# Quotients of cross attention's outputs formed by POOL behind its subtraction, DVE's block transpose of them near the end of its slot

## The reference

```python
def _L0_xattn_ref(Q, K, V, mask, Wq, bq, Wk, bk, Wv, bv, Wo, bo):     # 16 heads of 8
    q = _split(Q @ Wq.T + bq, N_HEAD)
    k = _split(K @ Wk.T + bk, N_HEAD)
    v = _split(V @ Wv.T + bv, N_HEAD)
    score = jnp.einsum('bhqd,bhkd->bhqk', q, k) * scale
    score = jnp.where(mask == 0, -jnp.inf, score)
    attn = jax.nn.softmax(score, axis=-1)
    out = jnp.einsum('bhqk,bhkd->bhqd', attn, v)
    B, H, S, dh = out.shape
    out = out.transpose(0, 2, 1, 3).reshape(B, S, H * dh)
    return out @ Wo.T + bo
...
x = x + _L0_xattn_ref(_layernorm(x, axis=-1), ctx_1024, ctx_1024, mask, ...)   # x: (128, 32, 128), ctx: (128, 257, 128)
```

## Time and profile before

| | |
|---|---|
| median of 3 runs | 1475.41 us (1472.41 to 1478.68) |
| the profiled execution | 1479.32 us, its span 1477.5 us, granted clock 0.948 of full |
| cross attention in it | POOL's first subtraction starts at 63.29 us, its last at 476.94 us |
| PE busy | 1314.1 us, 89% |
| DVE busy | 1195.3 us, 81% |
| ACT busy | 1113.4 us, 75% |
| POOL busy | 716.2 us, 48% |

### The profile page before, as it was taken

How to read it: one execution, slowest core, us unless ns; L and a number is a source line. 1 busy time by engine, 2 the same in 40 slices (tenths; PEclk the granted TensorE clock), 3 DMA queues, 4 the chain that set the end, 5 groups by cost and what they waited for, 6 DMA issues and landing times.

```text
span 1477.5 us, 45922 instructions
## 1 busy us (share of the span) xinstructions
PE 1314.1 (89%) x15671; PEld 997.7 (68%) x15671; DVE 1195.3 (81%) x3413; ACT 1113.4 (75%) x1877; POOL 716.2 (48%) x557
## 2 busy tenths in 40 slices
PE   5898999999978799679788798999999998998988
PEld 3676778777766688537566566666767666666666
DVE  4799899899997689678886886878787878687885
ACT  3698999999967567368767676778787787677776
POOL 7276777787769445514322232343444433233323
PEclk9999999999986699789989999999999999999999
DMA  6876676677642688100000000000000000000000
GB/s 162 220 209 164 185 193 179 186 193 186 176 117 66 171 211 213 36 1 2 1 0 0 0 2 1 0 0 0 0 0 0 0 0 1 2 7 14 7 14 15
DMA packets 196200, 108.45 MB, mean 73 GB/s; under 512 B 89740, under 2 KB 194028, under 8 KB 196076
## 3 DMA queue, kind: packets, MB, share of 16 engines
q1 hardware_dynamic: 122032, 84.65, 20.9%
q10 hardware_dynamic: 74044, 22.17, 6.8%
HBM read 67.62 MB, written 39.03 MB: 72 GB/s over the span
## 4 chain that ended last, share of the span: by engine, by line
DVE 20%; PE 15%; issue 12%; ACT 5%; DVEq 1%; ACTq 0%
PE pair L1739 7%; PE pair L1721 6%; DVE hs L1652 4%; ACT gf L1594 3%; ACT gh L1599 2%; DVE xc L1626 2%; DVE rs L51 1%; PE pair L1751 1%; DVE rs L53 1%; DVE gl L1638 1%; DVE st L1617 1%; DVE rs L49 1%; DVE rs L38 1%; DVE mv L1621 1%; PE pair L1728 1%
## 5 line engine op out<-in xcount | busy, mean ns | idle before, releaser
L1581 POOL TENSOR_TENSOR gl<-gf,gh 128x1024 f16<-128x1024 f32 x128 | 289.9, 2265 | 554.2 <-ACT gh L1599 554.2
L1594 ACT ACTIVATE gf<-pair,b1c 128x512 f32<-128x512 f32 x512 | 327.1, 680 | 151.9 <-PE pair L1721 151.7
L1739 PE MATMUL pair<-w2p,gh 128*128 (+1 forms) x4096 | 369.0, 222 | 9.0 <-DVE gl L1638 9.0
L1739 PE MATMUL pair<-w2p,gl 128*128 (+1 forms) x2048 | 360.0, 222 | 0.0
L1739 PEld LDWEIGHTS pair<-w2p,gh 128*128 128x128 f16 x4096 | 328.2, 100 | 35.1 <-issue 7.8
L1721 PE MATMUL pair<-xh,w1p 128*128 128x512 f16 x1024 | 328.7, 382 | 3.0 <-DVE w2p L1368 2.9
L404 POOL TENSOR_TENSOR pl<-p,ph 128x1024 f16<-128x1024 f32 x128 | 272.8, 2131 | 119.3 <-ACT ph L461 119.1
L1599 ACT ACTIVATE gh<-gf 128x1024 f16<-128x1024 f32 x256 | 270.6, 1057 | 25.5 <-ACT gf L1594 2.4
L1638 DVE SCALAR_TENSOR_TENSOR gl<-gf,gh 128x1024 f16<-128x1024 f32 x128 | 167.7, 1310 | 126.1 <-ACT gh L1599 124.0
L1739 PEld LDWEIGHTS pair<-w2p,gl 128*128 128x128 f16 x2048 | 204.3, 100 | 0.0
L1721 PE MATMUL pair<-xl,w1p 128*128 128x512 f16 x512 | 196.0, 383 | 0.0
(11 more groups left out here) (232 smaller groups left out, 2489.4 us busy)
## 6 DMA issues: line engine op xcount, KB each, us to landing
KS<-k_parts_dram SPq DMA_DIRECT2D x64, 384.0 KB, 4.5
k_parts_dram<-kh SPq DMA_DIRECT2D x64, 256.0 KB, 3.2
cx<-in_ctx_dram ACTq DMA_DIRECT2D x30, 512.0 KB, 4.5
k_parts_dram<-kl SPq DMA_DIRECT2D x64, 128.0 KB, 3.7
w1p<-in_L_ffn_w_dram SPq DMA_DIRECT2D x8, 512.0 KB, 5.9
w2p<-in_L_ffn_w_dram SPq DMA_DIRECT2D x8, 512.0 KB, 7.8
QS<-q_parts_dram ACTq DMA_DIRECT2D x128, 24.0 KB
Q<-q_parts_dram SPq DMA_DIRECT2D x32, 96.0 KB
```

What stands on the lines that cost most here:

```text
L1581: pool.tensor_tensor(gl[u.m2][:, 0:h, :], gf[u.m2][:, 0:h, :], gh[u.m2][:, 0:h, :], ALU.subtract).then_inc(d_loP, 1)
L1594: act.activation(gf[u.m2][:, c, :], hb[c][:, :], ACT.Gelu, scale=1.0 / WS, bias=b1c[:, u.step.expert(u.e), c]).then_inc(d_g, 1)
L1739: last = pe.matmul(yb[v.m2][:, t * D:(t + 1) * D], g[:, c, t * P:(t + 1) * P], w2p[:, le, part, c, :].rearrange("p a h -> p (a h)"), start ...
```

## The change

POOL gets one more instruction in each odd slot from 5 to 131: the quotients `on`, as a `tensor_tensor` multiply of the same tiles, placed behind its subtraction of the slot. DVE loses the quotients, and its block transpose of them moves from before the reduce to behind it. The computation is the same.

```diff
@@ POOL, slot s, behind pl
                         pool.tensor_tensor(pl[n % 4][:, :, :], p32[n % 2][:, :, :], ph[n % 4][:, :, :],
                                            ALU.subtract).then_inc(pl_done, 1)
+                    m = half(s - 5)
+                    if m is not None:
+                        pool.wait_ge(rec_done, m + 1)
+                        if m >= 2:
+                            pool.wait_ge(ot_done, m - 1)
+                        pool.tensor_tensor(on[m % 2][:, :, :, :], osum[m % 2][:, :, :, 0:DH],
+                                           orec[m % 2][:, :, :].unsqueeze(3).broadcast_to((P, 2, G, DH)),
+                                           ALU.mult).then_inc(on_done, 1)
@@ DVE
-                def quotients(m):
-                    dve.wait_ge(rec_done, m + 1)
-                    dve.scalar_tensor_tensor(on[m % 2][:, :, :, :], osum[m % 2][:, :, :, 0:DH], 1.0,
-                                             orec[m % 2][:, :, :].unsqueeze(3).broadcast_to((P, 2, G, DH)),
-                                             ALU.mult, ALU.mult).then_inc(on_done, 1)
...
-                    if m is not None:
-                        quotients(m)
                     if y is not None:
                         dve.wait_ge(y_read, y + 1)
                         dve.bn_stats(st2[:, y, :], xs[:, y, :]).then_inc(c_st, 1)
-                    if m is not None:
-                        transposed_quotients(m)
...
                         dve.tensor_reduce(mx[n // PB % 2][:, :, n % PB], RB[:, :].rearrange("p (g k) -> p g k", g=G),
                                           AX.X, ALU.max, negate=True).then_inc(r_read, 1)
+                    if half(s - 5) is not None:
+                        transposed_quotients(half(s - 5))
```

## The result

| | median us | lowest to highest | runs |
|---|---|---|---|
| before | 1474.42 | 1472.41 to 1478.68 | 4 |
| after | 1588.83 | 1585.90 to 1589.86 | 4 |

The account below looks back on a forecast made before the run. PE, ACT and DVE were nearly full; the wait that ends last decides, in a closed loop of one pair. Loop +90, layer norm steps +1 and end +7 made +98 us; against 1475.4 that gave 1574 us, range 1540 to 1630.

Parts of the forecast that it names:

- The wait and its place: DVE's transpose behind the reduce waits for POOL in every odd slot, 1.8 to about 2.8 us, some 100 to 150 in all.
- The loop: POOL's subtraction, DVE's low part of VX, PE's project_keys and scores, ACT's Exps form a closed turn: 8.28 us a pair, before 6.58.
- The price of the multiply: POOL's added 128x64 multiply per pair takes 0.31 us, between 0.22 and 0.47; those bounds change 53 turns by -5 or +8.
- The stretch to slot 110: Batch 5 to batch 111: 53 pairs take 438.8 us instead of 348.56, a difference of +90.3 us.
- small steps: Seven layer norm steps on DVE in slots 17, 19 and 21 come behind the transpose, about 0.2 us each: +1.
- the clock: Rival: TensorE's clock falls too as PE idles ahead of project_keys, +64 us, 1638, between 1600 and 1701; chance 0.12.
- The end: Slots 112 to 131, POOL the bound: added quotients and project_outputs waiting for the transpose cost +7 us, between 2 and 12.
- The bounds: Limits of the main case, from the multiply's time, layer norm steps in the turns used and the tail: about 1553 to 1592.
- the case without the clock: Main case: DVE's late low part of VX delays each turn while TensorE's clock stays at 1.00; 1574 us, chance 0.71.
- Absorbed: Rival: unseen slack takes up part of the delay, a turn costs 7.2 to 7.9 us, 1515 to 1553; chance 0.08.
- nothing: Rival: project_keys is not held by the late low part of VX, DVE's idle time takes the wait, 1475; chance 0.05.
- faster: Rival: DVE reaches the transpose only after POOL finished, and the saved 0.6 us shortens PE's waits by 16.4 us, 1459; chance 0.04.

Follow-up runs that it names:

- the wait alone: Kernel before, quotients and transpose in their old place, plus a DVE wait for POOL's subtraction behind each odd slot's reduce: 1553.4 us, 1.053.
- the added row scores: Changed kernel with PE doing the row scores of even slots 6 to 110 four times over, same result: 1570.6 us, 1.064 against the kernel before.
- tried alone: Changed kernel with POOL's multiply ahead of its subtraction up to slot 111 and behind it from slot 112 on: 1481.7 us, 1.005 against the kernel before.
- quotients ahead: Changed kernel with POOL's multiply ahead of its subtraction of the slot instead of behind it: 1467.5 us, 0.996 against the kernel before.
- the one with the clock at 0.95: Changed kernel with DVE's transpose behind the low part of VX, POOL's multiply still behind the subtraction: 1545.7 us, 1.049 against the kernel before.

## Why the prediction was right

- **The wait and its place.** Right. The transpose waits in every odd slot, 123.9 us from 80 to 520 us (100 to 150 foretold), and the wait alone, without any work moved, gives 78 of the 114 us. With the multiply ahead of the subtraction the loss is gone.
- **The loop.** Right at full clock. From the end of the subtraction to the end of the low part 1.18 us was foretold and 1.12 is seen; from there to the next odd subtraction 4.98 in a turn at full clock, as foretold. PE's wait at `project_keys` came in at 78.8 us, where some 110 were foretold: PE stands for 1.31 and 1.72 us in the turns shown and for 1.6 on the mean (78.8 in 50), since its row scores ahead of that point end later than I had reckoned (278.35 in the turn shown, 2.1 us after the subtraction's start). That does not touch the loop, as PE is waiting either way.
- **The price of the multiply.** Taken at 0.31, between 0.22 and 0.47; measured 0.295. Doubled, it shows 24.5 us.
- **The stretch to slot 110.** 8.28 us a pair and 1 us of small steps give +90 in 52.5 pairs; measured +103.2. Here the term at fault is the clock, which the sum had at nothing and which I had kept as a rival of its own with 0.12, "between 1600 and, at the worst, 1701". The prediction said that the clock should stay at 1.00 up to slot 111, and it named a reading of 0.50 between 80 and 500 us as a sign of being wrong. That reading came, in about every second turn and for some 3.5 us, with 0.65 us lost in the turn measured. With the clock kept up by the added row scores the same stretch is +85.9 (431.7 less 345.8), 4 less than foretold, and the whole kernel gets 18 us back, where the rival had 64. So the rival was true in its mechanism and small in its size; the two were not either-or. The row that I held against it, 118 to 140 us at 1.00, covers only three pairs.
- **The end.** Taken at +7, bounds 2 to 12; the traces show +12.1 against the kernel before, and 14.2 us when tried alone against quotients ahead. The mechanism was right but not complete: `project_outputs` waits for the transpose, and the outputs wait for `sums` besides. The size taken was about half of what came.
- **What followed.** The rest of the kernel was 5.1 us shorter in the profiled run (995.5 us from the last subtraction's start, against 1000.6). It holds the same work in all these kernels but for the last quotients. In nine of the ten experiments' profiles it took 991 to 997 us, and 1006.6 in the one with the clock at 0.95, so it is the 1000.6 that is long. No run ties the difference to the change.
- **The bounds.** The steps named add up to 1553 and 1587, not 1592 (1574 with 8 for the multiply and 5 for the end). Measured by the medians, 1588.8 is just above that: the case without the clock does not quite reach it.
- **Absorbed, nothing, faster.** None came. Of the faster case one part was right: it named the point that decides, whether POOL has the quotients before DVE asks. Moved ahead of the subtraction it has, and the kernel gets faster, but by 7 us and not by 16, and not in the loop.

The sum was +98 on the profiled execution; measured there, +110.4 (1589.7 less 1479.3), of which +17 is the clock (103.2 less 85.9). That the number came within 1% of 1574 is owed to the loop's arithmetic in the main, and in part to luck: the clock and the end were put too low, and the small overshoot of the loop and the shorter rest went the other way.

## What to carry to other kernels

Work handed to an idle engine is done when that engine's list comes to it. Before placing it, look at what the new owner is doing at the moment the result is asked for: POOL had 22% air (33.5 of 150 us), all of it ahead of its long instruction; the same multiply cost 114 us behind that instruction and gained 7 ahead of it. Then look at what stands behind the waiting instruction on its own list, since those are the ones that pay. And when a change gives PE a new stop in every turn (1.6 us on the mean here), count a fall of the clock as a term of the forecast, not as a separate case.

## What was not expected of the hardware

- TensorE's granted clock fell from 1.00 to 0.50 in a stretch where PE was busy for 354 of 440 us (81%), in about every second turn; in the kernel before it held 1.00 with 79% busy over 22 us. The Trainium skill (TensorE: Matmul & The Clock Gate, "HAM oscillation — how this bites in real kernels") describes this pattern, stops between groups of matmuls that send the clock down again and again. The trace agrees with the pattern, with 0.65 us lost in a turn, but not with the length of the stops: the page's are waits for a DMA of some 3 to 5 us, and no wait of PE was longer than 2.2 us from 80 to 520 us here.
- Added matmuls made a kernel faster: 1588.8 to 1570.6 us, with PE busy 400.4 instead of 354.3 us in the same 440.
- DVE's quotients took 0.225 us at the median in the kernel with the wait alone, where 51 of the 64 met no running POOL arithmetic, against 0.674 before, where 60 of the 64 met one: two thirds of what they seemed to cost was waiting for POOL. The rule of the Trainium skill that a DVE instruction with two SBUF inputs contends with a GpSimd instruction that reads SBUF (SBUF — State Buffer, "Who interferes with whom") fits that. What the spared time was worth is another matter: nothing in the loop, as above.
